# Second routing of a two-layer kernel: the group tables move behind the last one-hot block, and the slots' gates are summed behind the first tile's projection

## The reference, cut to what matters

```python
route = jax.nn.sigmoid(x @ Wr + br)
max_prob = jnp.max(route, axis=1, keepdims=True)
max_ind = jnp.argmax(route, axis=1)
for e in range(n_experts):
    mask = (max_ind == e)[:, None].astype(x.dtype)
    y = jax.nn.gelu(x @ W1[e], approximate=False) @ W2[e]
    out = out + mask * y
out = out * max_prob
```

## Time and profile before

| | us |
|---|---|
| median of 3 runs | 1730.97 |
| lowest, highest | 1727.98, 1731.4 |
| the profiled execution's own time | 1730.75 |
| its span | 1729.0 |
| PE busy | 1521.6 (88%) |
| DVE busy | 1123.6 (65%) |
| POOL busy | 1217.6 (70%) |
| ACT busy | 905.8 (52%) |
| the second routing, from DVE's first logits to the first matmul of a second expert | 1475.87 to 1502.81 |
| the second experts, to the end | 1502.81 to 1729.0 |

### The profile page before, as it was taken

The page is one execution under the profiler, slowest core; times in us unless marked ns, Lnnn a source line. Parts: engine busy times, 40 slices in busy tenths (PEclk is TensorE's granted clock), DMA queues, the critical chain, the costliest instruction groups (busy, mean ns, idle before and its releaser), DMA issues.

```text
span 1729.0 us, 38207 instructions
## 1 busy us (share of the span) xinstructions
PE 1521.6 (88%) x13596; PEld 1140.2 (66%) x13596; DVE 1123.6 (65%) x1786; ACT 905.8 (52%) x2305; POOL 1217.6 (70%) x1024
## 2 busy tenths in 40 slices
PE   6799999986899999999999967777887767699998
PEld 5466665655788888888888843333333226599998
DVE  7888989887343433333445557999999998533333
ACT  6678787843343444343444345545555446354553
POOL 4757777732476676676778627999999996366664
PEclk9899999995799999999999977989999887599999
DMA  6014444418344445545465460011111255388885
GB/s 220 20 41 131 130 145 128 128 37 318 82 116 106 120 104 118 123 100 122 120 171 155 100 215 23 1 31 32 30 42 43 92 176 175 138 264 251 262 264 152
DMA packets 148049, 217.34 MB, mean 126 GB/s; under 512 B 48904, under 2 KB 108576, under 8 KB 142752
## 3 DMA queue, kind: packets, MB, share of 16 engines
q1 hardware_dynamic: 115296, 132.26, 23.7%
q0 software_dynamic: 32576, 82.63, 19.9%
HBM read 143.23 MB, written 71.61 MB: 124 GB/s over the span
## 4 chain that ended last, share of the span: by engine, by line
PE 58%; POOL 20%; DVE 9%; issue 5%; DMA 4%; ACT 1%; POOLq 0%; DVEq 0%; ACTq 0%; SPq 0%
PE ps L832 54%; POOL BIG L2575 17%; DVE BIG L1426 4%; DMA BIG<-HB,BIG 3%; PE ps L953 1%; DVE BIG L2059 1%; PE ps L1134 1%; POOL BIG L2760 1%; POOL BIG L2759 1%; DVE bnst L1433 1%; POOL XD L2749 1%; PE ps L1203 1%; DMA XD<-BIG 1%; ACT BIG L2108 1%; POOL BIG L2737 1%
## 5 line engine op out<-in xcount | busy, mean ns | idle before, releaser
L832 PE MATMUL ps<-BIG 128*128 128x256 f16 (+9 forms) x11168 | 1224.3, 284 | 125.0 <-DVE BIG L2037 49.2
L832 PEld LDWEIGHTS ps<-BIG 128*128 128x128 f16 (+3 forms) x11168 | 936.2, 100 | 383.3 <-DVE BIG L2037 76.3
L2575 POOL TENSOR_TENSOR BIG<-BIG 128x256 f16<-128x256 f32 (+7 forms) x550 | 730.4, 1457 | 211.4 <-ACT BIG L2108 200.1
L2108 ACT ACTIVATE BIG<-BIG 128x512 f16<-128x512 f32 (+3 forms) x527 | 318.0, 662 | 233.2 <-DVE BIG L1426 176.2
L1426 DVE TENSOR_TENSOR BIG<-BIG 128x512 f16<-128x512 f32 (+10 forms) x347 | 259.8, 758 | 209.5 <-ACT BIG L2108 165.0
L2108 ACT ACTIVATE BIG<-ps 128x64 f32<-128x64 f32 (+7 forms) x663 | 232.1, 424 | 194.6 <-PE ps L1134 108.0
L1426 DVE TENSOR_TENSOR BIG<-ps,BIG 128x512 f32<-128x512 f32 (+3 forms) x389 | 284.8, 809 | 14.5 <-PE ps L832 13.1
L1426 DVE TENSOR_TENSOR BIG<-BIG,ps 128x512 f32<-128x512 f32 (+2 forms) x147 | 94.9, 645 | 187.4 <-PE ps L832 168.1
L2059 DVE TENSOR_REDUCE BIG<-BIG 128x160 f32<-128x2560 f32 x64 | 186.0, 2906 | 0.0
L2749 POOL DMA_INDIRECT XD<-BIG x67 | 113.2, 1690 | 85.9 <-DVE BIG L1943 82.1
L2737 POOL DMA_INDIRECT BIG<-HB,BIG x106 | 109.7, 1035 | 50.6 <-issue 27.0
(11 more groups left out here) (176 smaller groups left out, 1025.4 us busy)
## 6 DMA issues: line engine op xcount, KB each, us to landing
WD<-BIG SPq DMA_DIRECT2D x80, 256.0 KB
BIG<-in_v SPq DMA_DIRECT2D x32, 512.0 KB
BIG<-in_w SPq DMA_DIRECT2D x24, 512.0 KB
BIG<-WD SPq DMA_DIRECT2D x32, 384.0 KB, 7.9
HB<-BIG SPq DMA_DIRECT2D x64, 128.0 KB, 2.5
WG<-BIG SPq DMA_DIRECT2D x32, 256.0 KB
BIG<-WD SPq DMA_DIRECT2D x16, 512.0 KB, 5.2
XD<-X SPq DMA_DIRECT2D x32, 128.0 KB, 2.4
```

The source lines that it names most:

```text
L832: return e.matmul(o, lhsT, rhs, start=start, stop=stop, skip_group_check=True)
L2108: return e.activation(o, i, ACT.Copy)
L2575: return e.tensor_tensor(o, a, b, op)
```

## The change

Three things move in the second layer's part; the first layer's routing is as before. No operation is added or removed. On DVE the group tables are made behind block 3 rather than between blocks 1 and 2. On PE the 32 matmuls into `pp` leave the routing and come behind `up(0, 1)`. On DVE the two operations that make `PP` leave the routing's end and come behind the second `ut_lo` of tile 0; the experts' part now starts when `yi` is there.

```diff
@@ tensor, routing
                 if l == 0:
                     mod_columns(3)
-                else:
-
-                    for n in range(4):
-                        pe.wait_ge(s["rt"], rt_at[1, "AP", n])
-                        for r in range(8):
-                            m = mm(m_.pp, m_.S1[n][:, :, r], m_.AP[n][:, :, :, r], n == 0 and r == 0, n == 3 and r == 7)
-                    m.then_inc(s["pp_ps"], 1)
@@ tensor, second_experts
+                def gates_of_slots():
+
+                    for n in range(4):
+                        pe.wait_ge(s["rt"], rt_at[1, "AP", n])
+                        for r in range(8):
+                            m = mm(m_.pp, m_.S1[n][:, :, r], m_.AP[n][:, :, :, r], n == 0 and r == 0, n == 3 and r == 7)
+                    m.then_inc(s["pp_ps"], 1)
+
...
                     up(j, 0)
                     up(j, 1)
+                    if j == 0:
+                        gates_of_slots()
                     if j + 2 < NS:
                         turn(j + 2)
@@ vector, routing
                 for u in range(4 * CH):
-                    if l and u == 2:
-                        experts_of_groups()
...
-                if l == 0:
-                    experts_of_groups()
+                experts_of_groups()
                 dve.wait_ge(s["mp_ps"], at(l, "mp_ps") + 4 * CH)
...
-                else:
-                    dve.wait_ge(s["pp_ps"], 1)
-                    n = c.next()
-                    e.tensor_copy(m_.PP, m_.pp[:, 0, :]).then_inc(n, 1)
-                    n = c.next()
-                    tt(m_.PP, m_.PP, m_.pp[:, 1, :], ALU.add).then_inc(n, 1)
-                    rt_at[l, "PP"] = c.n
+                return c
@@ vector, second_experts
-                dve.wait_ge(s["rt"], rt_at[l, "PP"])
+                dve.wait_ge(s["rt"], rt_at[l, "yi"])
...
                            ut[0][:, 4 * hf:4 * hf + 4, :].rearrange(FLAT), ALU.subtract).then_inc(s["ut_lo"], 1)
+                    if j == 0:
+                        dve.wait_ge(s["pp_ps"], 1)
+                        n = c.next()
+                        e.tensor_copy(m_.PP, m_.pp[:, 0, :]).then_inc(n, 1)
+                        n = c.next()
+                        tt(m_.PP, m_.PP, m_.pp[:, 1, :], ALU.add).then_inc(n, 1)
+                        rt_at[l, "PP"] = c.n
+                        dve.wait_ge(s["rt"], c.n)
                     if j:
                         gated(j - 1)
```

More of the change, by code:

```diff
@@ L1964, in first_experts, with second_experts @@
                     down(t)
-            def second_experts():
+            def second_experts(c):
                 l, m_ = 1, M[1]
-                dve.wait_ge(s["rt"], rt_at[l, "PP"])
+                dve.wait_ge(s["rt"], rt_at[l, "yi"])
                 for w in rows_stored(l):
@@ L2098, in vector @@
                 pre_tick(1, t)
-            routing(1)
-            second_experts()
+            second_experts(routing(1))
         def scalar(e):
```

## The result

The changed kernel took 1734.68 us (median of 16 runs, 1731.44 to 1738.87), the kernel before 1729.35 us on the same chips (16 runs, 1725.51 to 1735.35). The ratio is 1.0031, 95% interval 1.0022 to 1.0040: 5.3 us slower, between 3.8 and 6.9 by the interval. That is more than the 0.2% named in the prediction.

The account below looks back on a forecast made before the run. Behind 1502.81 the kernel's end was taken to be PE's sum of work. Tables -0.8, gate sums +4.8 and `PP` nothing gave +4.0 on the median 1730.97, so 1735.0 us; range 1730.8 to 1738.0.

Parts of the forecast that it names:

- The tables behind block 3: Start of the second layer: `mp` read 1.5 us earlier, gathers 0.87 us earlier; gain 0.8 us, bounds 0 and 0.9.
- I count no wait for it: Tile 0's projection would not wait for its `W1`, fetched at 1493.35 with 8.6 us to arrive.
- The sums at 4.8 us at either clock: The 32 gate matmuls behind tile 0's projection pay full time, 4.8 us, as stepped reading gains nothing from the clock.
- Rival 1: The moved gate sums halve at the high clock: +1.6 us, 1732.6 us; chance 0.25.
- Rival 2: The moved sums cost the high clock too, tile 1's projection paying up to 2.5 us more: +6.5, 1737.5 us; chance 0.20.
- Rival 3: Start gains all: gathers 1.5 us earlier, clock up earlier, sums halved; -0.1, 1730.9 us; chance 0.08 with a smaller mishap.
- Rival 4: Gathers queue behind `W1` for the whole 0.87 us: +4.8, 1735.8 us; upper edge of the forecast's 0.47.
- `PP` at nothing: Two DVE operations moved into tile 0 cost nothing; at most 0.4 us if `ut_lo` is late.
- A later wait changes by some microseconds: Sign that the prediction is wrong: a later PE wait for gathers, 0.9 us before, changes by some microseconds.

Follow-up runs that it names:

- e10: The kernel before with only the group tables moved behind block 3, run a second time: 1731.64 us beside 1731.71, ratio 0.9999.
- e1: The kernel before with only the group tables moved behind block 3, gate sums left in place: 1736.99 us beside 1737.10, ratio 0.9995.
- e6: The changed kernel plus 16 contiguous filling matmuls of 512 columns behind the sums into `mp`: 1737.89 us, ratio 1.0037 to the kernel before.
- e3: The kernel before plus 32 unread sums behind `down` of tiles 7, 15, 23, 31, weights and columns stepped or contiguous by group: 1743.69 us (1 run).
- e4: The changed kernel with `AP` laid out so PE reads contiguous columns and DVE reads `A0` stepped: 1738.26 us, ratio 1.0007 to the kernel before.
- e2: The kernel before with only the gate sums and `PP` moved, tables left between blocks 1 and 2: 1741.52 us, ratio 1.0029.
- e11: The changed kernel profiled once more, nothing altered, to see the clock: that execution took 1729.08 us.
- e9: `e7` with 25 fillers instead of 16, 2 more between the turns and 3 behind the register loads: 1731.75 us, ratio 1.0003 to the kernel before.
- e7: `e6` plus the contiguous `AP` of `e4`, its products made behind `yi`: 1731.95 us, ratio 1.0013 to the kernel before.

## Why the prediction was right

The forecast was 1735.0 us, slower by 4.0; measured were 1734.68 and +5.3 (3.8 to 6.9). That the time itself is met to 0.3 us is in part luck: the kernel before measured 1.6 us less than in the three runs that the forecast started from, and the change cost 1.3 us more than the sum said.

- **The tables behind block 3.** Right in its course: PE's hole closed, `mp` is read right behind the tables, POOL issues `W1` 0.85 us behind the cast's end and gather 1 at 1496.51. Counted from the first sum, that is 8.74 us where it was 9.70: 0.96 us earlier, against 0.87 forecast. Tile 0's projection starts 0.7 to 1.2 us earlier by the stages; the term was 0.8. One step was read wrongly: it is not tile 1's turn that decides the start now but gather 0, behind which tile 1's turn follows without a wait in both profiles. And no set of runs shows the 0.8 us as time: the gates alone cost +5.0, the whole change +5.3, and their intervals overlap.
- **"I count no wait for it"**, said of `W1`, held for `W1` and failed further down the queue: where tile 1's projection follows at once, tile 2's gather is late by 0.89 us (`e10`) or tile 3's by 0.88 (`e1`). I had worked out when the first two gathers land and not the third, on DMA engines that are 90% busy. In both profiles of the changed kernel the turns of tiles 2 and 3 start without a wait, as the moved sums stand ahead of them, so the sum of the prediction was not hurt; alone, the edit is worth nothing that can be told (`e1`, `e10`).
- **The sums at 4.8 us at either clock.** Right: 4.65 with the clock up (`e6`), and 5.6 less some 1 us of clock in `e3`. Choosing the attention's stepped matmuls as the nearest row decided it. `e3` adds that the columns' step does it. The rule of the Trainium skill (SBUF — State Buffer, the note on 16-byte lines) agrees in that the columns on a new line each cost 0.145 us a matmul, and 0.060 with the same weights and contiguous columns. The same note lets two-byte elements be stepped for free up to eight, and at exactly eight it was not free here. No other step was run, so the line is not told apart from the step. Rival 1, the halved sums, is excluded: with contiguous columns the sums do get cheap (`e4`), with the step never.
- **Rival 2, the clock.** Right in its mechanism for some executions: the clock fell in the sums of the changed kernel's first profile, and tile 1's projection took 5.00 us where it took 2.82, 2.2 more, of the rival's 2.5. In `e6` it fell only behind the sums, in tile 1's projection, and in `e2` and `e11` not at all. The forecast had given it 0.20 as a case of the kernel, and it is one of the execution. It may make the difference between +4.0 and the +5.3 of the runs; what share of the runs it strikes was not measured, and what decides on it in an execution stays open. The rule of the Trainium skill (TensorE: Matmul & The Clock Gate, the HAM clock gate) that a busy PE gets the full rate does not hold for this stretch: 100% busy by the records, and down to 0.50 in the third and fourth window after the change.
- **Rival 3** had the gathers 1.5 us earlier: they are 1 us earlier. **Rival 4**, gathers behind `W1` for the whole gain: excluded by the start, which is earlier. Its time, +4.8, would fit the runs as well as +4.0 does.
- **`PP` at nothing.** Right: the first of its two operations starts at 1513.94, and `down(0)` at 1517.2.
- **A later wait changes by some microseconds**: it does so, from 0.3 to 3.8 us over all profiles, but between executions of one kernel too (2.0 and 0.3 in the changed one). It is not the chip alone, as `e1` (3.8) and `e3` (0.3) ran on one chip; beyond that it stays open, and so does `e6`: its runs give +6.4 us by the ratio, its stages (14.24 and 12.12) +3.0 against the mean of before; its interval overlaps that of the changed kernel.

No version beats the kernel before: the two nearest to it, the tables alone and `e9`, are equal to it within 0.18%. What the gates' move would have needed is something that waits for their place: before, they stood in the shadow of a transfer at no cost.

## What to carry to other kernels

Work that an engine does in a stretch in which it would only wait for a transfer is free however inefficient it is; moved out of that shadow it costs its full time, so price it at the new place by the nearest row with the same access pattern and not by the row beside it. When a start is brought forward, follow the transfers past the first one that is waited for: here the third or fourth gather was late in its place. And where single microseconds count, compare stages over two profiles of each kernel before a difference is given to the change.

## What the hardware showed that I had not expected

- A matmul of 78 columns that are read with a step of 16 bytes takes 0.145 us at 1.2 and at 2.4 GHz; with the same weights and contiguous columns 0.060 us, with both contiguous 0.040 us (`e3`, at the high clock).
- The clock fell to 1.2 GHz inside such a stretch while PE was 100% busy, some 3 to 4 us behind the first of the sums, in three of the six groups of stepped sums that ran at the high clock (changed, `e3` twice). In `e6` it fell 0.5 us into the contiguous projection behind them, and in `e2` and `e11` it did not fall. It did not fall in contiguous sums (`e3` twice, `e4`, `e7`, `e9`). But stepped columns are not the only thing ahead of a fall: in `e7` it fell inside tile 0's contiguous projection, 0.7 us into it, after a stretch with PE busy 2.72 of 6.40 us.
- On DVE the group of nine operations with the eight products `AP` went from 2.16 to 5.18 us in `e4`, where `A0` is read with a step of 16 bytes and the gate, which was read along the innermost index, is the same for 39 elements in a row. Which of the two costs the time was not told apart. To move a step from PE's reads to DVE's was no gift.
